# A graph kernel on one Trainium2 core: the first convolution fetches all its message rows by one-hot products instead of fetching 344 of 784 chunks by GpSimd row gathers

## What is computed

```python
x = x + gcn(layernorm(x))      # two graph convolutions of width 8, then width 512
x = x + ffn(layernorm(x))      # gate, up (512 -> 1408), silu, down; ternary-quantized weights
x = x + mean_conv(layernorm(x))  # mean over in-edges of 512-wide rows, times W
x = x + moe(layernorm(x))      # 16 experts, capacity 468

def _gcn_conv(x, W, b, src, dst, norm):
    h = x @ W                  # first convolution: W is 512 x 8, so h has 8 columns
    msg = h[src] * norm[:, None]
    return segment_sum(msg, dst) + b
```

## Time and profile before

| | |
|---|---|
| median of the timed executions | 3361.59 us |
| the timed executions | 2, 3358.95 to 3364.22 us |
| span of the profiled execution | 5135.2 us |
| its granted TensorE clock, mean | 0.765 of full |
| busy of the span: TensorE, VectorE, ScalarE, GpSimd | 58%, 38%, 25%, 39% |
| instructions | 61590 |

### The profile page before, as it was taken

One profiled execution on the slowest core, in us unless ns is written; L12 is line 12 of the kernel. 1 busy time (PEld: TensorE's weight loads), 2 busy tenths in 40 slices (PEclk: granted clock), 3 DMA queues, 4 the chain that ended last, 5 costly groups with the idle time before them and its releaser, 6 DMA issues. The chain is left out here.

```text
span 5135.2 us, 61590 instructions
## 1 busy us (share of the span) xinstructions
PE 2982.4 (58%) x17153; PEld 2061.9 (40%) x17154; DVE 1973.4 (38%) x3813; ACT 1285.4 (25%) x2086; POOL 2000.5 (39%) x2038
## 2 busy tenths in 40 slices
PE   7511179631111000299989999956667666665789
PEld 7400068620000000177777777732232232322477
DVE  9300079750000000166666566632223223232366
ACT  3200057410000000144444444420011111111344
POOL 0377700037777777300000000035555455554244
PEclk9555589755555555599999999977888788887799
DMA  3101023210000000022333233345555556555465
GB/s 101 39 5 11 4 64 96 61 41 3 3 3 3 3 3 3 6 91 88 107 95 102 88 104 100 100 151 168 168 170 161 163 173 182 170 161 158 134 193 155
DMA packets 241523, 466.48 MB, mean 91 GB/s; under 512 B 77093, under 2 KB 107069, under 8 KB 241235
## 3 DMA queue, kind: packets, MB, share of 16 engines
q0 software_dynamic: 107264, 235.06, 17.4%
q1 hardware_dynamic: 133970, 227.93, 14.2%
HBM read 395.90 MB, written 73.45 MB: 91 GB/s over the span
## 5 line engine op out<-in xcount | busy, mean ns | idle before, releaser
L1971 POOL DMA_INDIRECT rows<-xn_rows,srcT x784 | 744.2, 949 | 665.4 <-DVEq L2441 440.7
L129 POOL DMA_INDIRECT msg_c<-hid_rows,srcT x744 | 770.0, 1035 | 245.0 <-issue 236.5
L2122 PE MATMUL pV<-rows,oh 128*128 x2240 | 645.5, 435 | 331.6 <-issue 262.2
L2122 PEld LDWEIGHTS pV<-rows,oh 128*128 x2240 | 238.7, 107 | 724.1 <-issue 576.2
L1197 PE MATMUL pG<-parts,los 128*128 128x200 bf16 x2640 | 308.6, 258 | 322.7 <-issue 322.7
L1487 PE MATMUL gates<-xT,wgu_hi 128*128 128x384 f32 (+1 forms) x1848 | 472.3, 377 | 39.2 <-ACT gate_sum L1585 20.6
L1954 POOL IOTA bases<- 128x49 f32 x1 | 0.2, 188 | 1269.8 <-POOLq L387 1269.8
L1518 PE MATMUL accs<-wd,hT 128*128 128x512 f32 x1617 | 405.4, 398 | 16.2 <-DVE hT L1733 16.2
L129 POOL DMA_INDIRECT msg_b<-hid_rows,srcT x344 | 345.5, 1004 | 110.2 <-issue 105.6
L1197 PEld LDWEIGHTS pG<-parts,los 128*128 128x128 bf16 x2640 | 240.9, 100 | 356.0 <-issue 354.2
L1487 PEld LDWEIGHTS gates<-xT,wgu_hi 128*128 128x128 f32 x1848 | 336.4, 190 | 105.4 <-issue 60.9
(11 more groups left out here) (432 smaller groups left out, 5300.1 us busy)
## 6 DMA issues: line engine op xcount, KB each, us to landing
wd<-wd_rows SPq DMA_DIRECT2D x154, 512.0 KB
we<-in_L_ffn_expert_w SPq DMA_DIRECT2D x16, 1024.0 KB
lo<-lo_rows SPq DMA_DIRECT2D x110, 128.0 KB
x_rows<-xr SPq DMA_DIRECT2D x49, 256.0 KB, 4.0
xn_rows<-pair SPq DMA_DIRECT2D x49, 256.0 KB
rows<-xn_rows,srcT POOLq DMA_INDIRECT x784
res<-x_rows SPq DMA_DIRECT2D x49, 256.0 KB
x_rows<-agg SPq DMA_DIRECT2D x49, 256.0 KB
```

Of the source, the lines that this page charges most:

```text
L129: nc.gpsimd.indirect_dma_start(msg[:, c, :], None, table, bass.IndirectOffsetOnAxis(ap=srcT[:, c:c + 1], axis=0)).then_inc(landed[u % 2], 16)
L1971: nc.gpsimd.indirect_dma_start(rows[:, u % RING, c, :], None, xn2_rows, bass.IndirectOffsetOnAxis(ap=srcT[:, u * Q + c:u * Q + c + 1], axi ...
L2122: last = nc.tensor.matmul(pV[:, ds(to, 1), :].rearrange("p a d -> p (a d)"), oh[:, ds(to, 1), c, :].rearrange("p a d -> p (a d)"), rows[:, ...
```

## The change

`M` becomes C // 4 = 196, so all 784 chunks go through the one-hot products. The 344 indirect DMAs of stage B, the table `hid1_rows`, its store at the end of stage A and the semaphores `landed`, `hid1` of that path are gone. `MB` becomes 4 (196 is not a multiple of 5), and the buffers `picked`, `prest` take 16 chunks instead of 20. `MW` becomes 6 and `MD` 14: the 22 `wide` pieces take groups 0 to 131, the `down` pieces start at groups 133, 147, 161 and 175. Stage C keeps its own constant `MC` and its gathers.

```diff
--- before.py
+++ after.py
@@ -40,20 +40,20 @@
 assert CQ * Q == C and all(n * BY_Q >> 16 == n // Q for n in range(C))
 BY_T = -(-(1 << 17) // NT)
 assert all(n * BY_T >> 17 == n // NT for n in range(NT * P)) and (NT * P - 1) * BY_T < 1 << 24
-M = 110
-MB = 5
-MW = 3
-MD = 10
+M = C // 4
+MB = 4
+MW = 6
+MD = 14
 AHEAD = 3
 LR = 4
 LB = 6
 LC = 6
 OUTSIDE = -2.0 ** 122
 HT = -(-NT // 2)
-assert 4 * M * P <= E and 4 * M % V == 0 and M % MB == 0 and 4 * MB == U
+assert 4 * M == C and M % MB == 0 and MB >= 4
 assert (HT - 1) * -OUTSIDE < 2.0 ** 127
 MC = 10
-assert 4 * MC % V == 0 and MC <= M
+assert 4 * MC % V == 0
 CN = CQ + NT + 1
 DX = max(CX, CN * Q)
 RING = 4
@@ -397,7 +397,6 @@
         hi_rows = dram("hi_rows", (C, P), BF16)
         lasts = dram("lasts", (1, NT), F32)
         x3_rows = dram("x3_rows", (NT * P, XW), F32)
-        hid1_rows = dram("hid1_rows", (NT * P, H3), BF16)
         hid2_rows = dram("hid2_rows", (NT * P, H), F32)
         x2_rows = dram("x2_rows", (NT * P, D), F32)
         xn2_rows = dram("xn2_rows", (NT * P, 2 * D), F16)
@@ -515,10 +514,6 @@
                 sp.dma_start(hi_rows.rearrange("(p c) q -> p (c q)", p=EP), high_b[:]).then_inc(s["ext_out"], 16)
                 sp.wait_ge(s["ext_out"], 64)
 
-                sp.wait_ge(s["hid1"], 1)
-                sp.dma_start(hid1_rows.rearrange("(p t) f -> p t f", t=NT), packed[:]).then_inc(s["stored"], 16)
-                sp.wait_ge(s["stored"], 16)
-
             @block.gpsimd
             def _(pool):
                 own = Steps(pool, s["pool"])
@@ -680,7 +675,6 @@
                 dve.wait_ge(s["h_used"], G)
                 own.step(nc.vector.tensor_tensor(hid[:], h1[:], bc(dinv[:].unsqueeze(2), (P, NT, H)), ALU.mult))
                 split3(nc, own, packed, hid, hrest)
-                dve.sem_inc(s["hid1"], 1)
                 own.step(nc.vector.tensor_copy(own3[:, 0:NT, 0:H3], packed[:]))
                 own.step(nc.vector.tensor_scalar_max(invdeg[:], pD[:, 0:NT], 1.0))
                 own.step(nc.vector.reciprocal(invdeg[:], invdeg[:]))
@@ -805,7 +799,6 @@
         wd_in = sem("b_wd_in")
         lo_in = [sem(f"b_lo_in{j}") for j in range(LB)]
         hi_in = [sem(f"b_hi_in{j}") for j in range(LB)]
-        landed = [sem(f"b_landed{h}") for h in range(2)]
         with ExitStack() as ctx:
             msg = sb(ctx, "msg_b", [P, CX, H3], BF16)
             sc = sb(ctx, "sc", [P, 3, FB], F32)
@@ -817,8 +810,8 @@
             nw = sb(ctx, "bnw", [P, NT], F32)
             rest = sb(ctx, "rest", [P, 2, NT * H], F32)
             sq = rest[:, 0].rearrange("p (t f) -> p t f", f=H)
-            picked = sb(ctx, "picked", [P, 2, U, H], F32)
-            prest = sb(ctx, "prest", [P, U, H], F32)
+            picked = sb(ctx, "picked", [P, 2, 4 * MB, H], F32)
+            prest = sb(ctx, "prest", [P, 4 * MB, H], F32)
             sig = sb(ctx, "bsig", [P, 1], F32)
             number = sb(ctx, "number", [1, CN], F32)
             lanes = sb(ctx, "lanes", [P, 4], F32)
@@ -932,7 +925,6 @@
                 nc.gpsimd.iota(number[:], [[1, CN]], base=0, channel_multiplier=0, allow_small_or_imprecise_dtypes=True).then_inc(s["numbered"], 1)
                 nc.gpsimd.memset(msg[:, C:CX, :], 0.0).then_inc(s["tail"], 1)
                 pool.wait_ge(s["tail"], 1)
-                gather_units(nc, pool, hid1_rows, srcT, msg, landed, s["msg"], 4 * M // V)
                 pool.sem_inc(s["msg"], U // VS)
 
             @block.vector
@@ -998,7 +990,7 @@
                 def split_picked(q, m):
 
                     value = picked[:, q % 2]
-                    part = [msg[:, q * U:(q + 1) * U, j * H:(j + 1) * H] for j in range(3)]
+                    part = [msg[:, q * 4 * MB:(q + 1) * 4 * MB, j * H:(j + 1) * H] for j in range(3)]
                     if m == 0:
                         dve.wait_ge(s["reduced"], (q + 1) * MB)
                     if q > 0 or m > 0:
```

## The result

The changed kernel takes 3498.7 us in the median of two executions (3497.8 to 3499.6), against 3361.6. The ratio is 1.0405, with a 95% interval from 1.0384 to 1.0426: 137 us slower. The forecast was 171.5 us slower, with a range from 3430 to 3575 us; the time lies in it.

What follows compares the result with a forecast made beforehand. The prediction took stage B's groups of products as the bound, with gathers almost hidden: +194.1 - 11 - 10.6 - 1 = +171.5 us on 3361.6 gives 3533 us (+5.1%), range 3430 to 3575.

Steps and rivals of the forecast that it cites:

- The stall in the trace was the recording's: Stages with gathers: engines idle beside them only when recorded; nearly all of 1774 us absent from the timed execution.
- the sum of time: Whole kernel: timed 3361.6 us against profiled 5135.2; stretches without gathers can't shrink by much, so those with gathers must.
- the timeline: Start of stage B: TensorE runs at full pace for the first 8 us of gathers, then stalls per instruction.
- 86 more groups on the path: Stage B's fetch: all added groups of products lengthen the path, +194.1 us with the gain from spread weight pieces included.
- line 988: VectorE step in stage B's fetch: 0.50 us beside gathers, 0.34 without; removing the gathers saves 10.6 us.
- The spreading: Stage B's fetch: weight pieces every six groups instead of three make TensorE the bound, worth -12.3 us.
- Gathers are hidden but for 11 us: End of stage B: removing 344 gathers gives back only the late landing of the last, 11 us (0 to 22).
- gathers were the end of the stage: Rival for stage B: gathers at 1.38 us land 30 us later than assumed, giving 3503 us; chance 0.10.
- Stage D's bound: Stage D's 1083 us of timed execution allow at most 1.38 us a gather; used to limit stage B's pace.
- Store of `hid1_rows`, 1 us: Between stages A and B: dropping the store saves 1 us, between 0 and 3.8.
- The real stall: Rival for stage B: gathers truly stall TensorE's and VectorE's issue; up to -157 us, 3205 us; chance 0.10.
- Mild slowing: Rival for stage B: gathers slow the products in timed execution; all 103 us there give 3441 us; chance 0.12.

Runs made afterwards that it cites:

- second trace: Kernel of before, unchanged, executed and profiled again: 3365.9 us, ratio 1.0001, span 3366.4 us.
- the row of M: Kernel of before (M = 110) with other M: 120 took 3324.4 us, 120 with spread pieces 3322.0, 124 with spread pieces 3332.2; the changed kernel is M = 196.
- the numbers in PSUM: Kernel of before with line 213's first operand in stage B's tile loop read as float32 from PSUM: 3358.2 us, ratio 0.9987.

## Why the prediction was right, and by how much it was off

*The stall in the trace was the recording's.* Right. Of all later executions of the kernel before, none was near 5135 us, and its second trace has none of the stall. Two of the three reasons held, the sum of time and the timeline. The third, that over half of the records were lost and the recording overloaded, did not: the second trace has 107,264 packets too, without a stall. The prediction took 128 packets for a gather, but stage B's count 32 each: the pages with and without all 344 differ by 107,264 - 96,256 = 11,008 = 344 x 32, and with 304 the page has 105,984, which is 304 x 32 more than 96,256. Whether a packet stands for four rows or only every fourth is recorded is not shown, but it is the same with the stall and without. So the conclusion was right with one wrong reason beside it, and the cause of the stall stays open.

*86 more groups on the path, and line 988.* Right within 12 us: 194.1 - 10.6 = 183.5 forecast, 194.9 measured, as line 988's share is in the measured length of before. The fetch before took 316.8 us where 310.3 + 10.6 = 320.9 was taken, after 511.7 where 504.4 was. The second gap, 7.3 us, is that of the 22 wide pieces, each 0.34 us longer than forecast (7.5 us); why they are was not found. Line 988's term was mis-sized: gathers cost the fetch 3.2 us instead of 10.6. It had been taken from single rows of the stalled recording; in the second trace the median of line 988 is 0.345 us beside gathers, and 0.344 in the kernel without them. 2.40 us a group is confirmed by the row of M.

*The spreading.* 12.3 forecast, 9.5 and 9.6 measured.

*Gathers are hidden but for 11 us.* This is the step that was mis-sized, and it holds the error of the forecast. The mechanism was there (the stage ends with the last gather when they are slow), as a term of 11 us and as the rival "gathers were the end of the stage", which gave 3503 to the measured 3498.7. It measured 63.4 us. The prediction took 1.29 us for every gather, also in the tile loop. In the second trace the 236 gathers of the fetch came 1.34 us apart, which makes 12.3 us, and the 47 in step with line 213 came 2.00 apart, which makes 33.6: together the 45.7 us by which the last one started later than 641. The loop alone would be done at 626.3 instead of 630. Stage D's bound of 1.38 us a gather did not cover this: in the second trace stage D's gathers came 1.29 us apart and stage C's 1.33, so neither stage shows what stage B's loop does to them. The recording of before could not show it: its gathers were all done before the loop began.

The rival's 3503 lies so near by luck. It had 41 us of late landing for the measured 63.4. Half of the 22 us that it lacked was made up for by the fetch, which it had too short by 11.4 us, and the medians differ by some 6 us more than the spans.

*Store of `hid1_rows`, 1 us.* Right. From the last splitting step of stage A to stage B's first copy on VectorE it is 192.03 - 187.64 = 4.39 us in the second trace of before and 183.15 - 179.50 = 3.65 without the store:

```profile
187.64 0.56 DVE L2633 CAST packed<-hrest 128x392 bf16<-128x392 f32 x1
...
192.03 4.25 DVE L1018 COPY parts<-own 128x200 bf16<-128x200 bf16 x6 [1.93 <-PEq L387]
```
```profile
179.50 0.56 DVE L2625 CAST packed<-hrest 128x392 bf16<-128x392 f32 x1
...
183.15 4.24 DVE L1010 COPY parts<-own 128x200 bf16<-128x200 bf16 x6 [1.30 <-PEq L387]
```

That is 0.7 us. The other 8 us by which stage B begins earlier arise before the store, where the kernels do not differ: the last splitting step starts at 187.6 in the second trace of before, at 179.7 in the kernel without gathers and at 171.9 in the one with M = 120, which all have the store, and at 179.5 in the changed one. So stage A varies by that much from one trace to another.

So the forecast was 11.4 us too low in the fetch and took 52.4 too little for what the end of the gathers gives back: 171.5 + 11.4 - 52.4 = 130.5, beside the 131.5 by which the spans differ and the 137 of the medians. That the two errors go against each other, and that stage A's 8.9 us less stand against stage C's 11.9 more, is luck; of the last two the prediction had only the 1 us of the store.

*The real stall* (0.10) is refuted: with no gathers at all the kernel of before gains 58 us (about 65 by the estimate above), not 190. *Mild slowing* is refuted by the same run. *The clock* was 0.99 in the fetch after.

## What to carry to other kernels

When two engines share a job in front of a loop, the split that matters is the one at which both are done when the loop needs their last piece: here ten groups more on TensorE's side (120 of 196) helped by 1%, and all of them there cost 4%. Price the second engine beside each stretch that it runs in, not with its pace in one of them. And when a span is half as long again as the timed execution, compare the sums of stages before believing a stall, and take a second trace.

## What was not expected of the hardware

A gather on GpSimd's queue takes 0.94 us alone, 1.67 beside a VectorE tensor_tensor of 1.49 us with both inputs in SBUF, and 0.94 beside one of 2.82 us with one input in PSUM. Next to a memset of 7.35 us on GpSimd a VectorE tensor_scalar of 0.34 us took 7.39.

Stage C's FFN took 1225 to 1248 us from its first to its last `gates` matmul in the traces without the stall, without a change in its code: 1226.7 and 1225.2 in the kernels of before with and without gathers in stage B, 1232.4 with the numbers in PSUM, 1239.1 in the changed one, 1239.8 with gathers put back, 1248.4 with its pieces close together, 1237 to 1240 with M = 120 and 124. That is up to 23 us which no edit explains, and it stays open. With one trace a kernel it can't be told whether the longer FFN of the six kernels with more groups is chance or comes with them. The rows of that stretch, of before in its second trace and of the changed kernel with its pieces close together:

```profile
777.00:2003.70 1226.70, 1133.62 (x6208) 923.43 (x6209) 751.57 (x1531) 577.58 (x964) 700.97 (x693) 0.98 0.36 97
```
```profile
909.70:2158.10 1248.40, 1144.82 (x6208) 931.64 (x6209) 751.65 (x1531) 578.25 (x964) 702.42 (x693) 0.97 0.34 95
```

The numbers of instructions agree. Of the 21.7 us that the second is longer, 11.2 are busy time of TensorE and 10.5 its idle time. The granted clock is 0.98 in the first and 0.97 in the second; it is 0.98 in the two kernels with 1225 to 1227 us and 0.97 in all the others. Whether the clock makes the stretch longer or the waits lower the clock was not tested.
